# A running-sum chain with a semaphore of its own, and an increment of the shared one once per four columns

## What is computed

```python
def _gcn_layer(x, src, dst, norm, W, b, n_nodes):
    h = x @ W
    msg = h[src] * norm[:, None]
    out = jax.ops.segment_sum(msg, dst, num_segments=n_nodes)
    return out + b
...
x = x + _L0_gnn_ref(_layernorm(x, axis=-1), edge_index, ...)
x = x + _L0_ffn_ref(_layernorm(x, axis=-1)[None], ...)[0]
```

## Time and profile before

| | us |
|---|---|
| median of 3 runs | 10736.66 |
| lowest and highest | 10717.01, 10742.34 |
| span of the profiled execution | 10757.3 |
| running sums, layer 0 (first to last start) | 266.1 to 2594.6 |
| running sums, layer 1 | 2866.1 to 5032.7 |
| running sums, layer 2 | 5307.0 to 7473.7 |
| attention and experts, about | 7480 to 10757 |

### The profile page before, as it was taken

One profiled execution on the slowest core, in us unless ns is written; L12 is line 12 of the kernel. 1 busy time (PEld: TensorE's weight loads), 2 busy tenths in 40 slices (PEclk: granted clock), 3 DMA queues, 4 the chain that ended last, 5 costly groups with the idle time before them and its releaser, 6 DMA issues.

```text
span 10757.3 us, 49102 instructions
## 1 busy us (share of the span) xinstructions
PE 2354.0 (22%) x10310; PEld 1918.9 (18%) x10310; DVE 3773.2 (35%) x7766; ACT 1979.6 (18%) x3186; POOL 6413.3 (60%) x6399
## 2 busy tenths in 40 slices
PE   1122000000300000000300000000635556665664
PEld 0111000000300000000300000000524445554553
DVE  4556655543333333332333333333501111111125
ACT  1111111111411111111311111111301111111112
POOL 4655666676477777776477777776473443333343
PEclk9999999998655555555655555555857677777787
DMA  4444555555555555555555555555621111111126
GB/s 134 158 158 167 174 180 179 177 197 169 177 192 187 187 187 187 187 187 170 168 193 187 187 188 187 187 187 178 198 49 44 35 32 45 45 43 40 45 72 182
DMA packets 589401, 1573.35 MB, mean 146 GB/s; under 512 B 137512, under 2 KB 378388, under 8 KB 550484
## 3 DMA queue, kind: packets, MB, share of 16 engines
q1 hardware_dynamic: 302196, 877.99, 22.6%
q0 software_dynamic: 285488, 678.64, 21.9%
q10 hardware_dynamic: 1584, 15.48, 0.4%
HBM read 810.67 MB, written 760.96 MB: 146 GB/s over the span
## 4 chain that ended last, share of the span: by engine, by line
DVE 14%; PE 13%; another core or an unknown queue 11%; issue 11%; POOL 1%; DMA 1%; ACT 1%; SPq 0%; DVEq 0%; POOLq 0%; ACTq 0%
DVE ps L1215 12%; PE ps L1642 6%; PE ps L1653 6%; POOL acc L1083 1%; PE ps L1690 1%; DMA onehot<-feature_table 0%; ACT work L1705 0%; DVE work L1244 0%; DVE acc L1254 0%; PE ps L1165 0%; DVE stats L1260 0%; ACT acc L1768 0%; DMA x_normed_t<-keep_within_node 0%; DVE acc L2031 0%
## 5 line engine op out<-in xcount | busy, mean ns | idle before, releaser
L1083 POOL DMA_INDIRECT acc<-feature_table,staged_indices x4608 | 4689.0, 1018 | 2148.5 <-issue 1596.4
L1215 DVE SCALAR_TENSOR_TENSOR ps<-ps,keep_within_node,acc 128x256 f32<-128x256 f32 x4692 | 2310.1, 492 | 3589.7 <-DVE ps L1215 1432.6
L1545 POOL DMA_INDIRECT acc<-attention_table,idx x1024 | 986.2, 963 | 1445.5 <-DVEq L1841 1134.9
L1003 ACT COPY acc<-ps 128x1024 f32<-128x1024 f32 x787 | 796.9, 1013 | 3782.4 <-DVE ps L1215 3280.5
L1127 PE MATMUL ps<-work,carry_from_partition 128*128 128x256 f32 x4 | 2.4, 714 | 4400.9 <-ACT work L1003 4400.9
L1642 PE MATMUL ps<-work 128*128 128x256 f32 x3136 | 801.8, 401 | 706.1 <-issue 519.5
L1800 DVE TENSOR_TENSOR acc<-ps,acc 128x512 f32<-128x512 f32 x196 | 135.6, 692 | 2177.8 <-DMA onehot<-feature_table 1022.1
L1653 PE MATMUL ps<-work,onehot 128*128 128x256 f32 x3136 | 763.0, 391 | 345.2 <-issue 331.1
L1127 PEld LDWEIGHTS ps<-work,carry_from_partition 128*128 128x128 f32 x4 | 1.0, 311 | 4401.8 <-ACT work L1003 4401.8
L1642 PEld LDWEIGHTS ps<-work 128*128 128x128 f32 x3136 | 627.9, 201 | 855.2 <-issue 572.3
L1705 ACT ACTIVATE work<-ps,eb_sb 128x256 f32<-128x256 f32 x784 | 307.7, 475 | 2200.3 <-remote 1161.6
(11 more groups left out here) (393 smaller groups left out, 3020.1 us busy)
## 6 DMA issues: line engine op xcount, KB each, us to landing
unning_features_of_edges<-acc SPq DMA_DIRECT2D x195, 2048.0 KB
unning_features_of_edges<-work SPq DMA_DIRECT2D x96, 2048.0 KB
acc<-feature_table,staged_indices POOLq DMA_INDIRECT x4608
expert_rows<-acc SPq DMA_DIRECT2D x196, 256.0 KB
onehot<-feature_table SPq DMA_DIRECT2D x147, 256.0 KB
feature_table<-acc SPq DMA_DIRECT2D x98, 256.0 KB
acc<-attention_table,idx POOLq DMA_INDIRECT x1024
work<-expert_rows SPq DMA_DIRECT2D x14, 1024.0 KB
```

Of the source, the lines that this page charges most:

```text
L1003: nc.scalar.copy(sums_out[slot][:, 4 * j:4 * j + w].rearrange("p c f -> p (c f)"), ps[:, b:b + 2].rearrange("p a f -> p (a f)")[:, 0:w * D ...
L1083: nc.gpsimd.indirect_dma_start(out=rows_in[r][:, k], out_offset=None, in_=table, in_offset=bass.IndirectOffsetOnAxis(ap=staged[:, r, k:k + ...
L1215: nc.vector.scalar_tensor_tensor(state[k % HELD], state[(k - 1) % HELD if k else before], keep1[:, c + k:c + k + 1], rows_in[r][:, k], ALU ...
L1545: nc.gpsimd.indirect_dma_start(out=rows[:, i % 2, c], out_offset=None, in_=gat_table, in_offset=bass.IndirectOffsetOnAxis(ap=idx[1][:, sta ...
```

## The change

DVE gets a second semaphore for each layer, `column_summed` (`s_sum`). The memset and every running sum add 1 to it instead of to `columns_summed`, and DVE's waits before a column go to it. DVE's sequencer adds 4 to `columns_summed`, once per group of four, at the second column of the next group, after its wait for the first column of that group and before the second column's instruction. After the last column it waits for that and adds the last 4. The thresholds of ACT and POOL are adapted: ACT's for a group is `begun + (4 * U + 4 * j + w)`, POOL's for a chunk is `m * U + U`. Since the last group of a chunk is announced at the second column of the next chunk, POOL's condition holds one column later than before; ACT's holds at the same column as before. Each layer has 391 such increments.

```diff
@@ layer
             s_carry, s_fixd = sem("carries" + n_), sem("fix_done" + n_)
+            s_sum = sem("column_summed" + n_)
@@ on_scalar, copies_of
-                        act.wait_ge(s_c, begun + (4 * U + 2 + 4 * j + w - (size == LAST[-1] and j == groups(size) - 1)))
+                        act.wait_ge(s_c, begun + (4 * U + 4 * j + w))
@@ on_gpsimd, gather
-                    pool.wait_ge(s_c, m * U + (U + 1))
+                    pool.wait_ge(s_c, m * U + U)
@@ on_vector
-                nc.vector.memset(state[HELD - 1], 0.0).then_inc(s_c, 1)
+                nc.vector.memset(state[HELD - 1], 0.0).then_inc(s_sum, 1)
...
-                        dve.wait_ge(s_c, 4 * U + c + k + 1)
+                        dve.wait_ge(s_sum, c + k + 1)
+                        if k % 4 == 1 and c + k > 1:
+                            dve.sem_inc(s_c, 4)
                         nc.vector.scalar_tensor_tensor(
                             state[k % HELD], state[(k - 1) % HELD if k else before], keep1[:, c + k:c + k + 1], rows_in[r][:, k],
-                            ALU.mult, ALU.add).then_inc(s_c, 1)
+                            ALU.mult, ALU.add).then_inc(s_sum, 1)
...
                     before = (size - 1) % HELD
+                dve.wait_ge(s_sum, C1 + 1)
+                dve.sem_inc(s_c, 4)
```

## The result

The changed kernel takes 10753.17 us (median of 20 runs, 10744.36 to 10763.55) against 10735.28 us of the kernel before beside it (20 runs, 10717.01 to 10749.33). The ratio is 1.0017 with a 95% interval of [1.0011, 1.0023]: 18 us longer, within 0.3%. A repeat in a later series gave 1.0019 [1.0010, 1.0028]. The forecast was +10 us, 10747 us, with a range of 10610 to 10875.

The account below looks back on a forecast made before the run. The prediction took DVE's late increment to bound layers 1 and 2, and DVE's chain with the sort's PE and ACT layer 0. Terms 0 + 10 + 0 + 0 = +10 us gave 10747 us, range 10610 to 10875.

Parts of the forecast that it names:

- Part 1: Sums' increments moved to the private semaphore: priced at 0, a private chain being as late as the shared one.
- The first rival: The shared semaphore caused the delay, so all layers speed up: 10285 us, or down to 9955; chance 0.13.
- the late increment of DVE: Layers 1 and 2: the wait that ends last, 22.4 us a chunk for what costs POOL 20.0.
- Part 2, layers 1 and 2 swallow the step: Sequencer's 0.11 us steps vanish in the wait for rows or in the 0.70 us steps; cost 0.
- third rival: Slow chunks of layers 1 and 2 move by one 0.70 us step: 10614 or 10870 us; chance 0.07 each way.
- Part 2, layer 0 pays about 10 us of the steps: Layer 0: about a quarter of 391 sequencer steps at 0.11 us lie open, 10 us, bounds 0 and 43.
- Part 3: ACT's copy of a group, released by the sequencer's increment up to 0.11 us later: cost 0.
- Part 4: POOL's wait for the chunk four back, met one column later, hides behind the staged-indices wait: cost 0.
- The second rival: Each added increment takes its own 0.70 us step in slow chunks of layers 1 and 2: 493 us, 11230; chance 0.08.

Follow-up runs that it names:

- e3_sp_loads: Changed kernel, but in layers 1 and 2 SP loads each chunk's rows by one transfer from consecutive rows, without POOL's gathers; 8473.52 us, one execution.
- e8: e6 with an increment on one DVE instruction of three instead of two, the other one's wait kept only at a chunk's first pair; 10951.65 us, ratio 1.0164.
- e9: Changed kernel with a tiny DVE copy behind each sum, without increment or wait; 11039.47 us, ratio 1.0240 to the kernel before.
- e7_layers_1_2: The change in layers 1 and 2 alone, layer 0 as in the kernel before; 10739.74 us, ratio 1.0000.
- e1: Kernel before, chain on the shared semaphore, with only the sequencer's added step, onto a semaphore nobody waits on; 10766.81 us, ratio 0.9993.
- e10: The kernel of e1 run once more, against the kernel before; 10773.87 us, ratio 0.9998.
- e11: Changed kernel with POOL's notice of a chunk one column earlier, as before the change, through its own semaphore; 10802.19 us, ratio 1.0024.
- e2: Changed kernel with the sequencer incrementing the old semaphore by 1 at every column instead of 4 at every fourth; 10846.22 us, ratio 1.0065.
- e6: Changed kernel with sums taken two columns at a time, three DVE instructions per pair, half the dependent steps; 10853.86 us, ratio 1.0103.
- e5: Changed kernel with each column's sum split into two halves, each a chain with its own semaphore; 10942.16 us, ratio 1.0194.

## Why the prediction came out right, and where it didn't

**Part 1, the private semaphore is worth nothing: right, shown for layers 1 and 2; in layer 0 it wasn't tried alone.** The first rival (10285 or less) is out: the chain waits alone on its semaphore and layer 1 takes 2166.4 us. The reason given, that the earlier trace rows show a private chain just as late, held; e3_sp_loads confirms the other half of it, that the gathers are what the slow places share. What the late thing is was put wrongly. The prediction speaks of the late increment of DVE. e8 and e9 show that the time goes by the number of instructions, with or without an increment, and the earlier trace rows could have told it: 0.18 us of work and 1.22 of idle time are 1.40. For this change the two give the same time, since it leaves the number of sums alone.

**Part 2, layers 1 and 2 swallow the step: right, shown** by e7_layers_1_2 at 1.0000. Fast chunks grew by 0.48 us (0.44 forecast) into the wait for rows. That wait isn't 11.5 us after each of the first nine chunks, as the prediction has it, but shrinks from the fifth on, to 1.4 us after the ninth; that is still more than the 0.44, so the cost of 0 stands. Slow chunks kept 22.4 us on average, but not each of them: in layer 1, 45 chunks take 22.4, 22 take 21.7 and 21 take 23.1, where before 85 took 22.4. This is the third rival's pattern, which the prediction lists as a sign of being wrong, moving by one step to either side; since the moves cancel, it costs nothing. The prediction gave it the whole sum of one sign, 123 us, and didn't see that it could alternate. (Its 10614 is counted from 10737 and its 10870 from 10747, so one of them is off by 10 us.)

**Part 2, layer 0 pays about 10 us of the steps: right in place, wrong in cause, and lucky in size.** The price is 17 us and all in layer 0 (e7). But the step alone costs nothing (0.9993 and 0.9998), against the sentence that a quarter of the 391 steps lie open. That is the term that failed: it should have been 0, and the 17 us belong to something that the sum doesn't have.

**Part 3, ACT's release at no cost: open, one of its reasons wrong.** It is one of two differences left when the step (e1, e10) and POOL's notice (e11) are taken out; the other is part 1's private semaphore in layer 0. The prediction let the copy be hidden because the columns that need its place come four or eight later; in layer 0 the nearest comes three after the release. Even so it was hidden: the copy had ended at least 0.60 us before that column. Which of the two makes the price, and by what wait, no run shows.

**Part 4, POOL's wait hidden behind the staged indices: right.** The timeline has POOL start 2.10 us after ACT's copy, 2.11 before, and e11 brings nothing back.

**The second rival** (each increment takes a place of 0.70) is out for the sequencer's steps: e2 has 12 more a chunk for two more places. It turned out true for something nobody had added, whole DVE instructions, which take two places each. Had the change added one DVE instruction a column instead of a step of the sequencer, it would have cost 2.4%.

The Trainium skill's rule (VectorE: DVE Perf Modes, "The DRAIN you can't avoid"), that a semaphore after each DVE operation costs nothing extra, agrees with e6 against e8 in the slow chunks, where 16 or 9 increments give the same 33.6 us.

**Open:** how the change costs layer 0 its 17 us; what the 0.70 us is; and why a slow stretch ends. In e5, e6, e8 and e9 each return from slow to fast chunks in layers 1 and 2 comes after POOL had been held back for space by 6.4 us or more, while in the kernel before and the changed one POOL never pauses there for more than 0.9 us and no slow stretch ends. That the pause is the cause wasn't tried. Nor can these runs tell whether the recording of the instructions has a part in it, since none without it is known.

## What to carry to other kernels

When a chain on DVE is late beside POOL's indirect gathers, count its instructions before looking at its semaphores: here each cost 1.40 us in the slow regime, so splitting, pairing or adding instructions lost 1 to 2.4%, although the fast chunks of the split chain had every wait hidden. Steps of DVE's sequencer (a wait with an increment for another engine) are a cheap way to announce: 0.11 us where columns run fast and nothing where they don't, as long as they are few (twelve more a chunk cost 1.4 us). And before giving a chain a private semaphore, look in the trace for a chain that has one already: for layers 1 and 2 it told the answer here. When a small change costs something, take it apart before explaining it: the step that seemed to fill the price was free.

## What the hardware showed beyond this

- In e6's slow chunk the next pair started only after 1.6 to 4.9 us of idle time behind three instructions that had started 0.40 us apart; and instructions that waited for nothing (line 820 of the kernel before) were held to one per 1.40 us.
- POOL need not be slowed by it: in e6's slow chunk its gathers keep 0.95 us and 1.25 us of pace; in the changed kernel's some stretch, to 1.24 and 1.39.
- As many rows by SP's transfers instead of POOL's gathers (with the stores) moved 395 GB/s, and DVE ran each chunk through in 8.93 us.
- Two interleaved half-width chains hide the wait between dependent instructions: 0.26 us a half, 0.52 a column, against 0.53 for the whole column in one instruction.
